# A two-layer block on one Trainium2 core: x1 enters the row buffer through its high and low parts, with the first phase reordered

## What is computed

```
W(codes, scales)  = NF4[codes], each block of 64 inputs times its scale
lin(x, W, A, B)   = x W^T + (x A^T) B^T                        # LoRA, rank 16
attn = (lin_q(x) + lin_k(x) + lin_v(x)) / 3
x1   = x + lin_o(attn)
h    = silu(lin_gate(x1)) * lin_up(x1)                         # 1792 wide
F(x) = x1 + lin_down(h)
```

## Time and profile before

| | us |
|---|---|
| median of 3 runs (533.67 to 535.50) | 535.43 |
| the profiled execution | 534.0 |
| its span | 532.1 |
| TensorE busy | 494.5 (93%) |
| VectorE busy | 379.4 (71%) |
| ScalarE busy | 293.9 (55%) |
| GpSimd busy | 251.6 (47%) |

### The profile page before, as it was taken

One profiled execution on the slowest core, in us unless ns is written; L12 is line 12 of the kernel. 1 busy time (PEld: TensorE's weight loads), 2 busy tenths in 40 slices (PEclk: granted clock), 3 DMA queues, 4 the chain that ended last, 5 costly groups with the idle time before them and its releaser, 6 DMA issues.

```text
span 532.1 us, 7568 instructions
## 1 busy us (share of the span) xinstructions
PE 494.5 (93%) x2278; PEld 394.7 (74%) x2278; DVE 379.4 (71%) x716; ACT 293.9 (55%) x541; POOL 251.6 (47%) x252
## 2 busy tenths in 40 slices
PE   2968999788999999999999999899998899999995
PEld 0236678567888888888888888688886788888874
DVE  4888898666789789797987983577457966366442
ACT  6688856676666576666674742158487422332021
POOL 3357702465566576665674753147479410110001
PEclk9999999899999999999999999999999999999998
DMA  6575421243233333343333300740000000000011
GB/s 169 173 263 159 139 59 41 79 139 100 80 106 75 96 105 118 82 119 97 105 115 97 103 19 0 267 155 5 1 1 1 2 2 19 21 20 22 0 41 39
DMA packets 21415, 43.01 MB, mean 81 GB/s; under 512 B 3328, under 2 KB 3456, under 8 KB 21120
## 3 DMA queue, kind: packets, MB, share of 16 engines
q1 hardware_dynamic: 21152, 42.15, 25.6%
q0 software_dynamic: 224, 0.38, 0.3%
HBM read 40.42 MB, written 2.10 MB: 80 GB/s over the span
## 4 chain that ended last, share of the span: by engine, by line
PE 69%; ACT 3%; issue 3%; DVE 2%; POOL 0%; POOLq 0%; ACTq 0%; DVEq 0%
PE bank L996 62%; PE bank L1162 3%; PE bank L1009 2%; PE bank L1266 1%; ACT prob L957 1%; ACT pT_hi L780 1%; PE bank L1018 0%; DVE rmax L1480 0%; DVE pT_lo L1306 0%; ACT eb_hi L780 0%; ACT bank L785 0%; DVE rows L1413 0%; POOL gu_lo L740 0%; ACT v_hi L780 0%; PE bank L1025 0%
## 5 line engine op out<-in xcount | busy, mean ns | idle before, releaser
L718 POOL TENSOR_TENSOR wf<-value,scale 128x512 f32<-128x512 f32 x50 | 64.5, 1290 | 93.1 <-DVE value L1338 93.1
L996 PE MATMUL bank<-x_hi,gu_hi 128*128 128x512 f32 x224 | 89.9, 401 | 1.7 <-POOL gu_lo L740 1.7
L996 PE MATMUL bank<-x_lo,gu_hi 128*128 128x512 f32 x224 | 88.2, 394 | 0.0
L996 PE MATMUL bank<-x_hi,gu_lo 128*128 128x512 f32 x224 | 88.1, 393 | 0.0
L763 POOL TENSOR_TENSOR rstd<-veps,neg_half 128x1 f32<-128x1 f32 x32 | 17.6, 549 | 121.8 <-issue 110.5
L785 ACT ACTIVATE bank<-code 128x512 f32<-128x512 int32 x124 | 68.7, 587 | 0.0
L1316 DVE SCALAR_TENSOR_TENSOR low<-bent,bank 128x512 f32<-128x512 f32 x62 | 42.5, 685 | 24.0 <-ACT bank L785 19.4
L746 POOL TENSOR_TENSOR h_lo<-act_f,h_hi 128x512 fp32r<-128x512 f32 x28 | 36.3, 1297 | 31.7 <-ACT h_hi L780 31.7
L1413 DVE SCALAR_TENSOR_TENSOR rows<-bank,rows 128x512 f32<-128x512 f32 x48 | 33.0, 688 | 24.7 <-PE bank L996 24.3
L996 PEld LDWEIGHTS bank<-x_hi,gu_hi 128*128 128x128 f32 x224 | 42.6, 190 | 9.9 <-issue 2.1
L996 PEld LDWEIGHTS bank<-x_hi,gu_lo 128*128 128x128 f32 x224 | 42.5, 190 | 9.1
(11 more groups left out here) (198 smaller groups left out, 1172.7 us busy)
## 6 DMA issues: line engine op xcount, KB each, us to landing
code<-codes SPq DMA_DIRECT2D x62, 256.0 KB, 2.7
scale<-scales SPq DMA_DIRECT2D x100, 128.0 KB, 3.0
xs<-xT SPq DMA_DIRECT2D x2, 1024.0 KB, 5.6
ea_raw<-ex_A SPq DMA_DIRECT2D x1, 2048.0 KB, 9.9
eb_raw<-ex_B SPq DMA_DIRECT2D x1, 2048.0 KB, 7.5
out<-rows SPq DMA_DIRECT2D x8, 256.0 KB, 2.0
bgu_raw<-loB_gu SPq DMA_DIRECT2D x1, 896.0 KB, 4.7
wqkv_raw<-w_qkv SPq DMA_DIRECT2D x1, 768.0 KB, 4.3
```

Source lines behind the costliest of these rows:

```text
L718: pool.tensor_tensor(w, v, scale[:, i % RING_CODES, :], ALU.mult).then_inc(scaled_done, 1)
L996: last = nc.tensor.matmul(ps, a, b, start=start and i == 0 and n == 0, stop=stop and i == len(terms) - 1 and n == 2)
```

## The change

The diff does five things. The chunks' order becomes q0 k0 v0, the four o chunks, then the rest, with the items between them placed by three tables. An o chunk gets its LoRA by a merge on VectorE and is split like a gate chunk. The stacked LoRA factors are no longer made from padded loads: compact tiles `spread` are loaded, split once, written to two DRAM scratch tensors, and read back row group by row group into the stacked tiles, by SP, ahead of the codes of v3 (`stack_gu`) and of g1 (`stack_d`). x is loaded in eight pieces. And `xs` stays x: `rows` is loaded with x in rows, `res` brings the high and the low part of x1 through TensorE with an identity (`one_eye`, float32r) as the moving operand, eight matmuls for a tile, into bank 7, and VectorE adds the bank to `rows`. The identities are made by GpSimd in place of ScalarE.

The diff, cut:

```diff
-    chunks = [("o", k) for k in range(KT)] + [(m, i) for i in range(KT) for m in "qkv"]
+    chunks = [(m, 0) for m in "qkv"] + [("o", k) for k in range(KT)]
+    chunks += [(m, i) for i in range(1, KT) for m in "qkv"]
...
+BEFORE_CLIP = {
+    ("o", 2): [("acc", 0)], ("o", 3): [("merge", ("o", 1)), ("split", ("o", 1))],
+    ("q", 1): [("merge", ("o", 2)), ("split", ("o", 2))],
+    ("q", 2): [("m1", 0)], ("k", 2): [("acc", 1)], ("k", 3): [("acc", 2)],
+}
+BEFORE_OUT = {
+    ("o", 2): [("merge", ("o", 0)), ("split", ("o", 0))], ("q", 1): [("merge", ("o", 3))],
+    ("v", 2): [("m1", 1)], ("v", 3): [("m1", 2)],
+}
+AFTER_OUT = {
+    ("q", 1): [("split", ("o", 3))], ("k", 1): [("xsplit", 0)], ("v", 1): [("spread", 0)], ("q", 2): [("xsplit", 1)],
+    ("k", 2): [("spread", 1)], ("v", 2): [("xsplit", 2)], ("q", 3): [("xsplit", 3)], ("v", 3): [("xsplit", 4)],
+}
...
-        half(CHUNKS[j], 0)
-        if j == 0:
-            order.append(("eyes", 0))
-        half(CHUNKS[j], 1)
-        if j in XSPLIT_AFTER:
-            order.append(("xsplit", XSPLIT_AFTER.index(j)))
-    due.clear()
+        c = CHUNKS[j]
+        order.append(("mid", c))
+        order += BEFORE_CLIP.get(c, [])
+        order += [("clip", c), ("low", CHUNKS[j + 1])]
+        order += BEFORE_OUT.get(c, [])
+        order.append(("out", c))
+        order += AFTER_OUT.get(c, [])
     half(("g", 0), 0)
     half(("g", 0), 1)
+    order += [("acc", 3), ("xsplit", 5)]
+    half(("u", 0), 0)
     due.clear()
-    order += [("acc", 2 * KT - 1), ("bprep", 0), ("bprep", 1), ("m1", KT - 1)]
-    half(("u", 0), 0)
+    order.append(("xsplit", 6))
     half(("u", 0), 1)
     due.clear()
-    order += [("x1", 0), ("x1", 1), ("x1", 2), ("x1", 3), ("merge", ("g", 0)), ("x1", 4), ("split", ("g", 0))]
+    order += [("m1", 3), ("xsplit", 7)]
     half(("g", 1), 0)
-    order += [("x1", 5), ("merge", ("u", 0))]
+    order += [("x1", 0), ("merge", ("g", 0)), ("split", ("g", 0)), ("x1", 1), ("x1", 2), ("x1", 3)]
     half(("g", 1), 1)
-    order += [("x1", 6), ("split", ("u", 0)), ("x1", 7), ("dprep", 0)]
+    order += [("merge", ("u", 0)), ("split", ("u", 0)), ("x1", 4)]
+    due.clear()
     half(("u", 1), 0)
+    order += [("x1", 5), ("merge", ("g", 1)), ("split", ("g", 1))]
     half(("u", 1), 1)
+    order += [("x1", 6), ("merge", ("u", 1)), ("split", ("u", 1)), ("x1", 7)]
+    due.clear()
     half(("d", 0), 0)
-    order += [("silu", 0), ("res", 0)]
+    order.append(("silu", 0))
     half(("d", 0), 1)
     unit_h(0)
-    order.append(("res", 1))
+    order.append(("res", 0))
     half(("d", 1), 0)
-    order += [("silu", 1), ("res", 2)]
+    order += [("silu", 1), ("res", 1)]
     half(("d", 1), 1)
     unit_h(1)
-    order.append(("res", 3))
+    order.append(("res", 2))
...
+    if f == 2:
+        return [("res", TT - 1)] + downs_beside(f)[1:]
+    return [([None] + [("res", t) for t in range(TT)])[4 * f + i] for i in range(4)] if f < 2 else []
...
-            beside = [None, ("u", 1), ("d", 0), None]
+            beside = [None, ("d", 0), None, None]
...
+            x_before = {("o", 3): 0, ("q", 1): 1, ("k", 1): 2, ("v", 1): 3, ("k", 2): 4, ("v", 2): 5, ("q", 3): 6, ("k", 3): 7}
...
+            def wide(a):
+                return a.rearrange("(r c) e -> r c e", c=PIECES)
+
+            def long(a):
+                return a.rearrange("r (c e) -> r c e", c=PIECES)
+
+            def stack_gu():
+
+                sp.wait_ge(spreadhi_done, 1)
+                sp.wait_ge(spreadlo_done, 1)
+                sp.wait_ge(zeroed_v, 2)
+                cols = spread_cut(0)
+                sp.dma_start(scratch_hi[:, cols], spread_hi[:, cols].bitcast(F32)).then_inc(scratch_in, 16)
+                sp.dma_start(scratch_lo[:, cols], spread_lo[:, cols].bitcast(F32)).then_inc(scratch_in, 16)
+                sp.wait_ge(scratch_in, 32)
+                for i in range(3):
+                    a, b = (scratch_lo if i == 1 else scratch_hi), (scratch_lo if i == 2 else scratch_hi)
+                    for g in range(2):
+                        r = 32 * i + RANK * g
+                        sp.dma_start(long(la_gu[r:r + RANK, g, :].bitcast(F32)), wide(a[64 * g:64 * g + 64, 0:P]))\
+                            .then_inc(gu_rows_in, 16)
+                    sp.dma_start(long(lb_gu[32 * i:32 * i + 32, :].bitcast(F32)), wide(b[:, P:SPREAD_GU])).then_inc(gu_rows_in, 16)
+
+            def stack_d():
+
+                sp.wait_ge(spreadhi_done, 2)
+                sp.wait_ge(spreadlo_done, 2)
+                sp.wait_ge(zeroed_p, 2)
+                piece = FF // 2 // PIECES
+                cols = spread_cut(1)
+                sp.dma_start(scratch_hi[:, cols], spread_hi[:, cols].bitcast(F32)).then_inc(scratch_in, 16)
+                sp.dma_start(scratch_lo[:, cols], spread_lo[:, cols].bitcast(F32)).then_inc(scratch_in, 16)
+                sp.wait_ge(scratch_in, 64)
+                for i in range(3):
+                    a, b = (scratch_lo if i == 1 else scratch_hi), (scratch_lo if i == 2 else scratch_hi)
+                    for g in range(2):
+                        r, half = 64 * g + RANK * i, slice(64 * g, 64 * g + 64)
+                        sp.dma_start(long(la_dp[r:r + RANK, :].bitcast(F32)), wide(a[half, SPREAD_GU:SPREAD_GU + piece]))\
+                            .then_inc(d_rows_in, 16)
+                        sp.dma_start(long(lb_dp[r:r + RANK, g, :].bitcast(F32)), wide(b[half, SPREAD_GU + piece:]))\
+                            .then_inc(d_rows_in, 16)
+
             for j, c in enumerate(CHUNKS):
                 s = j % RING_CODES
-                if c == ("q", 1):
-                    sp.dma_start(xs[:, :, :SEQ], xT[:, :, :SEQ]).then_inc(x_in, 16)
-                if c == ("v", 1):
-                    sp.dma_start(bgu_raw[:, :], loB_gu).then_inc(bgu_in, 16)
-                    sp.dma_start(agu_raw[:, :, :], loA_gu).then_inc(agu_in, 16)
-                if c == ("q", 3):
-                    sp.dma_start(xs[:, :, SEQ:], xT[:, :, SEQ:]).then_inc(x_in, 16)
-                if c == ("k", 2):
-                    sp.dma_start(la_d[:, :], loA_d).then_inc(lorad_in, 16)
-                    sp.dma_start(lb_d[:, :, :], loB_d).then_inc(lorad_in, 16)
-                    sp.dma_start(low_rows[:, 1:4], stack_low).then_inc(lorad_in, 16)
+                if c in x_before:
+                    k, tk = x_tile(x_before[c])
+                    sp.dma_start(xs[:, k, tk], xT[:, k, tk]).then_inc(x_in[x_before[c]], 16)
+                if c == ("q", 2):
+                    sp.dma_start(spread[:, spread_cut(0)], lora_gu).then_inc(spread_in[0], 16)
+                    sp.dma_start(spread[:, spread_cut(1)], lora_d).then_inc(spread_in[1], 16)
+                if c == ("v", 3):
+                    stack_gu()
+                if c == ("g", 1):
+                    stack_d()
+                if c == ("d", 1):
+                    sp.wait_ge(gu_rows_in, 16 * 9)
+                    sp.wait_ge(d_rows_in, 16 * 12)
+                    for b in range(NB):
+                        sp.dma_start(rows[:, b * TPB:(b + 1) * TPB, :], x_rows[:, b * TPB:(b + 1) * TPB, :])\
+                            .then_inc(x_rows_in, 16)
...
-            pool.dma_start(sc_qkv[:, :, :], scales_qkv).then_inc(sqkv_in, 16)
             pool.dma_start(ident[:, :], eye).then_inc(eye_in, 16)
-            pool.dma_start(la_o[:, :], loA_o).then_inc(lora_in, 16)
-            pool.dma_start(lb_o[:, :], loB_o).then_inc(lora_in, 16)
             pool.dma_start(la_qkv[:, :], loA_qkv).then_inc(lora_in, 16)
             pool.dma_start(lb_qkv[:, :], loB_qkv).then_inc(lora_in, 16)
+            pool.dma_start(la_o[:, :], loA_o).then_inc(olora_in, 16)
+            pool.dma_start(lb_o[:, :], loB_o).then_inc(olora_in, 16)
+            pool.memset(la_dp[:, :].bitcast(F32), 0.0).then_inc(zeroed_p, 1)
+            pool.memset(lb_dp[:, :, :].bitcast(F32), 0.0).then_inc(zeroed_p, 1)
+            pool.wait_ge(eye_in, 16)
+            for to, factor in ((unit_eye, 1.0 / GAIN), (three_eye, 3.0 * GAIN), (gain_eye, GAIN), (one_eye, 1.0)):
+                pool.tensor_scalar(to[:, :], ident[:, :], factor, None, ALU.mult).then_inc(gain_set, 1)
...
+            pe.wait_ge(lora_in, 32)
+            slice_lora(0)
+            pe.wait_ge(olora_in, 32)
+            for k in range(KT):
+                nc.tensor.matmul(mm_ps[k][:, :], la_o[:, k * P:(k + 1) * P], lb_o[:, :], start=True, stop=True)\
+                    .then_inc(olora_ready, 1)
+            pe.wait_ge(gain_set, 4)
+            slice_sums(0)
+            pe.wait_ge(acchi_done, 1)
+            pe.wait_ge(acclo_done, 1)
+            slice_lora(1)
+            slice_m1(0)
+            for i in range(1, KT):
+                if i > 1:
+                    pe.wait_ge(m1hi_done, i)
+                    pe.wait_ge(m1lo_done, i)
+                    slice_lora(i)
+                slice_sums(i)
+                pe.wait_ge(m1hi_done, i)
+                pe.wait_ge(m1lo_done, i)
```

(37 more changed lines are left out.)

240 lines of the change are left out of this document (93 added, 147 removed).

## The result

The changed kernel took 541.74 us (median of 4 runs, 540.80 to 544.12), the kernel before 534.55 (4 runs beside them, 533.62 to 535.50). The ratio is 1.0141, with a 95% interval of 1.0100 to 1.0182: slower, by 0.2 us more than the high end of the range allowed, where the forecast was 535.0.

What follows compares the result with a forecast made beforehand. Vector-engine dequantization mostly leads up to the first gate product; TensorE should bound afterwards, its idles faults of order. Terms -1.6 + 6.6 - 5.5 = -0.5 us gave 535.0 us on the median's scale; range 526.5 to 541.5.

Steps and rivals of the forecast that it cites:

- part 2: LoRA factors through DRAM: stacks in SP's queue delay the codes of v3 and g1; +6.6 us, bounds 0 and 12.
- part 3: x1 without its float32 copy: +3.2 us of TensorE products, but waits behind the first gate product go; sum -5.5 us.
- The table of stages: Nothing changes from 127.39 us on; the whole question lies in the two stages before, split at the first gate product.
- Part 1: Order of the first phase: o sums leave TensorE for merges on VectorE; -1.6 us at the last slice sum.
- rival B: Reads cost SP about 0.6 us, writes land after 3.0, TensorE goes cold; 540.5 us, chance 0.17.
- 1.4 higher for both stacks: Addition to the DRAM-stack sum if, by the skill's fit, the two 295 KB writes took some 3.4 us.
- The clock: Lower TensorE clock after its idle before the last partial products: 0 to 1.9 us, taken as 0.9.
- rival A: SP's stacks are covered by a later vector chain, so they cost nothing; -7.1, 528.3 us, chance 0.30.
- C: The 64 residual-tile products don't pipeline, 0.16 us each instead of 0.10, 3.8 us more; 539 us, chance 0.08.
- D: TensorE reaches its upper clock level in the opening series, so the 3.5 us wait goes; 531.5 us, chance 0.08.
- The range: Whole kernel: 526.5 us (A with cheaper products and D's slack) to 541.5 us (B); the forecast's own, 532 to 538.

Runs made afterwards that it cites:

- a3: Changed kernel with both stacks' scratch writes sent earlier and their reads spread in groups between code loads; 528.81 us, ratio 0.9893.
- a4: Changed kernel with each of the 21 stack reads in place but taking plain two-dimensional rows (wrong LoRA factors); 537.23 us, ratio 1.0048.
- c2: a3 with part 3 undone (float32 transposes, ScalarE eviction, float32 sum of x1), residual tiles' slots kept; 532.46 us, ratio 0.9935.
- c1: Kernel before with nothing but part 3, residual tiles in their old slots; 535.59 us, ratio 0.9999.
- c4: c1 without VectorE's two remainders of the down factors (which changes the down LoRA term); 531.41 us, ratio 0.9936.
- d2: a3 with eight additions of no use on VectorE at the head of the stage; 532.71 us, ratio 0.9972.
- d1: a3 with only the eight additions of x1 into its float32 copy put back at their old place, result unused; 533.23 us, ratio 0.9982.
- b1: a3 with slice sum 0 made after the second of the four o LoRA pairs instead of the fourth; 529.41 us, ratio 0.9904.

## Why the prediction was wrong, step by step

**The step that failed** is the size of part 2. The stacks in SP's queue were put at +6.6 us, at most 12, and cost 12.9 between a3 and the changed kernel. With them spread the kernel gains 5.9 us, where the recorded sum without them was -7.1. A second step, the cause of part 3's gain, failed without showing in the time.

**The table of stages** was read rightly: what follows the end mark did not move (404.7 us in both), and the whole change lies in the two stages ahead of it.

**Part 1** held where it could be seen. TensorE starts at 8.17 (8.0 was recorded), the slice sum 0 is done at 21.1 (22.0), the three bubbles are 1.25, 1.23 and 1.23 (1.2 each), q1's value comes at 34.69 (35.2), k3's codes go out at 49.07 (48.8). VectorE's wait for that sum is 1.96 where 3.5 was recorded. Of the -1.6 at the last slice sum about -0.5 is left without the stalls (63.20 in a3 against 63.70).

**Part 2** had the right mechanism and every size too small, each from a row of another kind of transfer:

- A read of split rows was priced by a plain transfer, 0.47. It costs 0.65. The row that was alike stood in the same group, a broadcast scale pair in 1.10; rival B took it from there.
- The writes were priced by the tail's out transfers, 2.0. They land after 3.3 and 3.6 us in the first stack. The tail's DMA share is 0.10 (520 to 542 us), here it is 0.71 (49.5 to 53.5 us); that this makes the difference is not shown. From the first write to the first read SP spends 4.08 us in the first stack and 4.09 in the second, where 2.67 were recorded. The Trainium skill's warning ("DMA: Bandwidth & Descriptors", "Anatomy of one DMA") that the receipt of a write to HBM can take long points the right way, and the estimate of 3.4 us worked out from its fit is nearer than the 2.67, but still 0.7 short; by the same fit the second pair, of 176 KB each, would take 2.8 (an estimate), and it takes as long as the first. The recorded "1.4 higher for both stacks" used 3.4 for both.
- The codes behind a stack took 3.4 us to arrive in the first case and 2.8 in the second, where 2.7 was put.
- One read of the second stack held the queue for 1.51 us, and another is followed by a gap of 0.4; a4 shows such a read too, of 1.89. No run tells why.

So the stacks are 9.9 and 13.0 us long where 6.9 and 8.3 were recorded, and TensorE's waits 5.72 and 5.25 where they were 2.4 and 3.1. In the sum this is the largest miss but not the only one. **The clock** was put at 0.9 us. After the first wait the LoRA of the last slice takes 0.9 longer; and from its last slice sum the changed kernel needs 33.65 us to the first gate product, of which 5.25 are the wait and 24.05 what a3 needs without one (63.20 to 87.25): 4.4 more are the lower clock, 0.80 and 0.82 in the two windows above, where TensorE has no other idle. The account of the first gate product, recorded at 92.5 and measured at 103.71:

| step | recorded | measured | difference |
|---|---|---|---|
| last slice sum, with the first wait | 64.5 | 70.06 | +5.6 |
| second wait | 3.3 | 5.25 | +2.0 |
| lower clock behind the last slice sum | 0.9 | 4.35 | +3.4 |
| the rest of TensorE's path | 23.83 | 24.05 | +0.2 |
| together | 92.5 | 103.71 | +11.2 |

The 5.6 are 2.1 for a wait 4.5 longer than a3's 1.22 where 2.4 was put, 0.9 for the slower LoRA, and 2.5 for the walk: a3 comes to that LoRA 1.1 later than recorded (62.14 against 61.05), and this execution runs another 1.5 behind a3's from before the stacks. So the 11.2 are those of the slowest execution; the medians missed by 6.7 (541.74 against 535.0).

**Part 3** came out at the recorded number for a wrong reason. The stage was put at 34.4 and is 33.93, the tile at 0.80 and is 0.84. But c2 has the same length of stage without part 3, and c1 not with it. The sentence that failed is "That the waits go is the point: the eviction now stands on VectorE directly behind `h` 0": it stands on VectorE in c1 as well, and TensorE waits 3.29 for it; in c2 it is back on ScalarE, and the wait of 3.46 is gone. The +3.2 for the 64 products was right (3.3), and they fill waits that c2 still has. What shortens the stage came with parts 1 and 2, and the runs point to VectorE entering it with less to do: the first phase in the new order delivers one chunk more ahead of it (five values fall in the stage of a3 and six in that of c1), and the down factors' two remainders (2.43 us), which part 2 took off VectorE, are gone; c4 and d2 show from both sides that VectorE's load moves the wait. That it is the whole of it is argued, since c4 stops at 37.13, and how the rest divides between the new order and part 2 was not tried. And what part 3 does bring, 3.4 us by d1's profile, the prediction had set to 0.43: "its count stays". The count of VectorE's additions stays, but eight of them move to the stage, where it has room, six of these from ahead of the first gate product, where VectorE leads. In the kernel before they were covered: from the last slice sum to the first gate product c1 takes 23.26 us and the kernel before 23.83.

The two errors partly hid each other. The recorded sum for the changed kernel without SP's stalls, rival A, was 528.3, and a3 took 528.81; that is in part luck, as its 5.5 for part 3 came from the other parts.

**The rivals.** B was the case that came, at 0.17: reads of 0.6, writes after 3.0, a cold TensorE. It was priced at 540.5, with stacks of 9.0 and 10.8, and both came out longer. Its condition (above 0.53 us a read) was met, and a row of the profile met it in advance. C was wrong (0.11 a product and not 0.16). So was D: the first pairs run 1.8 to 1.9 us each, near the 2.0 of before and not the 0.96 of later ones, in a slice whose clock row shows 9. The Trainium skill's 81 ns for a load and a product of 128 columns ("TensorE: Matmul & The Clock Gate", "Back-to-back issue gap") is not what this stream shows: 110 ns, above the 100 taken from the LoRA row.

**The range** ended 1.0 above B's own sum, although both of B's stacks had been taken shorter than they came out; the result lies 0.2 above the range.

## What to carry to other kernels

Count what a step adds to an in-order queue of loads by the shape of each access pattern, take each price from a transfer of that shape under that load, and never let the queue wait for a landing in front of a load that somebody needs: send the writes early and put the reads, a few at a time, between the loads (a3, -12.9 us for no change in the work). Compare two profiles from an event behind the start that both have: here the start moved VectorE's walk by 1.6 us, as much as b1's edit brought. When an instruction is exchanged for one of the same length on the same engine, ask which of the two places is on that engine's critical stretch; the count says nothing. And a stage that gets as short as forecast does not show why it did: undo the part alone and do it alone before believing it.

## What the runs showed of the hardware

SP's queue took 0.46 us per issue of a DMA whose rows are plain (32 and 64 KB) and 0.64 to 0.65 where each row is cut into pieces, for 32 KB and for 224 KB alike. A float32r product of 128 columns with its own stationary tile took 0.11 us in a row of eight. A pair of writes of 288 KB each to DRAM landed 3.3 and 3.6 us after issue beside a load stream (DMA share 0.71), a pair of 176 KB after 2.8 and 3.5. After an idle of 5.72 us on TensorE the same float32 pair took 2.07 us instead of 1.13. In a profile the granted clock can read 1.00 where durations are those of the lower level: a3's first products of M1 are 0.43 us apart and later ones 0.23.
